# Token attention's last two units on VectorE, edge sends moved out of the last unit, feed-forward constants loaded ahead

## The reference, cut to what matters

```python
x = _layernorm(x + _L0_attn_ref(x, ...))        # attention across tokens
x = _layernorm(x + _L0_xattn_ref(x, ctx, ...))  # the two attentions below
x = _layernorm(x + _L0_ffn_ref(x, ...))         # feed-forward, 8 experts
x = _layernorm(x + _L1_attn_ref(x, ...))        # Nystrom attention, graph edges
x = _layernorm(x + _L1_xattn_ref(x, ctx, ...))
x = _layernorm(x + _L1_ffn_ref(x, ...))
```

```python
# 16 heads of 64, SCALE = 1/8, x1 the tokens, out = x1 + the first block on ctx
dots = jnp.einsum('bhid,bhjd->bhij', q, k) * SCALE
attn = jax.nn.softmax(dots, axis=-1)
out  = jnp.einsum('bhij,bhjd->bhid', attn, v)
return out @ Wo + bo
# feed-forward
x_attn = _layernorm(x_flat, ln_g, ln_b) @ attn_w + attn_b + x_flat
h = gelu(einsum(g, w1) + b1); y = einsum(h, w2) + b2
out = gelu(y @ next_w + next_b)
```

## Time and profile before

| | |
|---|---|
| median of 3 runs | 2498.34 us (2494.76 to 2500.62) |
| profiled execution | 2499.3 us, its span 2497.5 us |
| busy: TensorE, VectorE, ScalarE, GpSimd | 92%, 61%, 44%, 43% of the span |
| mean granted clock of TensorE | 0.956 of full speed |
| chain that ended last, largest part | TensorE 29% of the span |

### The profile page before, as it was taken

How to read it: one execution, slowest core, us unless ns; L and a number is a source line. 1 busy time by engine, 2 the same in 40 slices (tenths; PEclk the granted TensorE clock), 3 DMA queues, 4 the chain that set the end, 5 groups by cost and what they waited for, 6 DMA issues and landing times. The chain is left out here.

```text
span 2497.5 us, 34571 instructions
## 1 busy us (share of the span) xinstructions
PE 2295.9 (92%) x12918; PEld 1436.2 (58%) x12918; DVE 1520.1 (61%) x2287; ACT 1104.7 (44%) x2354; POOL 1079.6 (43%) x785
## 2 busy tenths in 40 slices
PE   6999999879988999998899999799899589979998
PEld 3333343356764555554555554688666467768887
DVE  6778678447745666764666666632444556666556
ACT  2667557723322444442344444233321457643233
POOL 2556546513443788883478888133301122100000
PEclk7889989999999999999999999899999699989999
DMA  6454333223110111112011111254201141010001
GB/s 131 114 97 87 70 65 76 77 57 62 1 18 1 10 15 14 15 31 39 1 14 11 15 15 14 80 133 126 61 25 45 32 115 52 1 64 14 1 1 34
DMA packets 137615, 114.22 MB, mean 46 GB/s; under 512 B 74501, under 2 KB 114931, under 8 KB 137065
## 3 DMA queue, kind: packets, MB, share of 16 engines
q1 hardware_dynamic: 100297, 111.08, 16.5%
q0 software_dynamic: 36864, 0.15, 4.4%
q10 hardware_dynamic: 288, 0.79, 0.2%
HBM read 85.99 MB, written 13.39 MB: 40 GB/s over the span
## 5 line engine op out<-in xcount | busy, mean ns | idle before, releaser
L345 POOL DMA_INDIRECT adj<-e_EE,e_IX x256 | 421.1, 1645 | 437.8 <-DMA adj<-e_EE,e_IX 346.5
L1799 DVE TENSOR_REDUCE c_MX<-PS 128x2 f32<-128x1024 f32 x256 | 312.9, 1222 | 175.6 <-PE PS L120 174.5
L124 POOL TENSOR_TENSOR c_AC<-c_AC,c_P 128x1024 f32<-128x1024 f32 x150 | 380.9, 2539 | 78.9 <-DVE c_AC L124 71.7
L1896 ACT ACTIVATE c_P<-PS 128x1024 f32<-128x1024 f32 x256 | 252.3, 1026 | 224.7 <-PE PS L120 216.6
L733 DVE TENSOR_REDUCE a_MX<-PS 128x2 f32<-128x1024 f32 x256 | 303.7, 1220 | 64.2 <-PE PS L120 61.9
L839 ACT ACTIVATE a_P<-PS 128x512 f32<-128x512 f32 x512 | 270.6, 601 | 95.9 <-PE PS L120 93.6
L120 PE MATMUL PS<-c_P,c_VV 128*64 128x512 f32 x1024 | 247.7, 605 | 0.0
L129 POOL TENSOR_SCALAR e_EQ<-e_KR,e_KC 128x128 bf16<-128x128 f32 x256 | 162.9, 636 | 160.9 <-DMA e_KR<-adj_key 125.1
L120 PE MATMUL PS<-a_QS,a_KS 64*128 64x512 f32 x512 | 197.4, 468 | 19.3 <-ACT a_P L839 8.5
L120 PEld LDWEIGHTS PS<-a_QS,a_KS 64*128 64x128 f32 x512 | 85.5, 193 | 174.4 <-ACT a_P L839 95.8
L120 PE MATMUL PS<-a_KS,a_QS 48*128 48x512 f32 x512 | 174.0, 482 | 11.6 <-DVE a_MX L733 4.6
(11 more groups left out here) (499 smaller groups left out, 4608.5 us busy)
## 6 DMA issues: line engine op xcount, KB each, us to landing
e_KR<-adj_key SPq DMA_DIRECT2D x64, 256.0 KB, 3.5
f_W<-in_L_ffn_w SPq DMA_DIRECT2D x16, 1024.0 KB, 6.9
c_RB<-c_r SPq DMA_DIRECT2D x58, 128.0 KB
g_FB<-in_fside_1x16xSxS SPq DMA_DIRECT2D x8, 616.0 KB, 8.0
a_QS<-a_QH SPq DMA_DIRECT2D x32, 128.0 KB
adj<-e_zt SPq DMA_DIRECT2D x16, 256.0 KB, 4.2
adj<-e_EE,e_IX POOLq DMA_INDIRECT x256, 3.2
d_AJ<-adj SPq DMA_DIRECT2D x8, 512.0 KB, 7.0
```

The lines of the kernel that those rows point to most:

```text
L124: return v.e.tensor_tensor(o, a, b, op)
L345: g.e.indirect_dma_start(self.adj, bass.IndirectOffsetOnAxis(ap=self.IXE[:, k:k + 1], axis=0), self.EE[:, k:k + 1], None, compute_op=ALU.a ...
L1799: v.e.reduce_max(MX[:, w % 2, :, qt, kh], bank(0, 2).rearrange("p (h n) -> p h n", h=2), AX, negate=True).then_inc(*smax_dve.up())
L1896: s.e.activation(PB[t % NP][:, :, :].rearrange("p h n -> p (h n)"), bank(2 + 2 * (t % 2), 2), ACT.Exp, scale=0.125).then_inc(*st_act.up())
```

## The change

- `lead(w)` gives 7 also for unit 30: VectorE makes all seven additions of units 15, 30 and 31. The additions 5 and 6 of unit 30 are placed at n = 0 and 1 of unit 31.
- The sum of unit 30 is made at n = 3 of unit 31 in place of n = 5, its scaling at n = 6 in place of 7.
- No sends in unit 31; one after each of `out` 9 to 15 instead.
- f_CR and f_AW now lie over LS and are loaded by SyncE at n = 6 of unit 31, once all queries have been prepared; `stage_f` allocates and loads neither.

```diff
     def lead(w):
-        return 7 if w % 16 == 15 else 2
+        return 7 if direct(w) else 2
...
-                    if n == 0 and not first:
+                    if n == 0 and not first and lead(w - 1) < 7:
                         yield "acc", w - 1, 7
+                    if w == 31 and n < 2:
+                        yield "add", 30, 5 + n
...
-                    if n == 7 and w == 31:
+                    if n == 6 and w == 31:
                         yield "scale", 30
+                        yield "fetch", 3
...
-                    if n == 5 and not first:
+                    if n == (3 if w == 31 else 5) and not first:
                         yield "sum", w - 1
...
-                    if n in (1, 3, 5):
+                    if n in (1, 3, 5) and w < 31:
                         yield "send", 1
...
         for t in range(9, 18):
             if t < 16:
                 yield "out", t
+                yield "send", 1
...
             elif kind == "fetch":
                 n, = a
-                if n == 1:
+                if n == 3:
+                    sp.wait_ge(q_pe, 32)
+                    K.consts.load(sp, A)
+                elif n == 1:
...
+class Consts:
+    def __init__(self, K):
+        self.CR = K.over("f_CR", "LS", 0, [84, 128], F32)
+        self.AW = K.over("f_AW", "LS", 512, [128, 2, 256], F32)
+        self.cr_in, self.aw_in = K.lasting(16), K.lasting(16)
+
+    def load(self, sp, A):
+        for place, name in ((slice(0, 64), "L0_ffn_b1"), (slice(64, 80), "L0_ffn_b2")):
+            dma(sp, self.CR[place, :], A[name].rearrange("e (f p) -> (e f) p", p=128)).then_inc(*self.cr_in.up())
+        for place, name in ((slice(80, 82), "L0_ffn_ln_g"), (slice(82, 84), "L0_ffn_ln_b")):
+            dma(sp, self.CR[place, :], A[name].rearrange("(f p) -> f p", p=128)).then_inc(*self.cr_in.up())
+        dma(sp, self.AW[:, :, :], A["L0_ffn_attn_w"].rearrange("(c p) n -> p c n", p=128)).then_inc(*self.aw_in.up())
...
-    AW = sb(c, "f_AW", [128, 2, 256])
-    CR = sb(c, "f_CR", [84, 128])
+    CR, AW = K.consts.CR, K.consts.AW
+    cr_in, aw_in = K.consts.cr_in, K.consts.aw_in
...
-        dma(sp, CR[0:64, :], A["L0_ffn_b1"].rearrange("e (f p) -> (e f) p", p=128)).then_inc(*cr_in.up())
-        dma(sp, CR[64:80, :], A["L0_ffn_b2"].rearrange("e (f p) -> (e f) p", p=128)).then_inc(*cr_in.up())
-        dma(sp, CR[80:82, :], A["L0_ffn_ln_g"].rearrange("(f p) -> f p", p=128)).then_inc(*cr_in.up())
-        dma(sp, CR[82:84, :], A["L0_ffn_ln_b"].rearrange("(f p) -> f p", p=128)).then_inc(*cr_in.up())
-        load("L0_ffn_attn_w", AW[:, :, :], aw_in)
```

More of the change, by code:

```diff
@@ L2040, in stage_f @@
     TM = sb(c, "f_TM", [128, 4, 256])
-    CR = sb(c, "f_CR", [84, 128])
     CC = sb(c, "f_CC", [128, 84])
-    aw_in, cr_in, rows_in, nw_in, ahead_in = [K.landing() for _ in range(5)]
+    CR, AW = K.consts.CR, K.consts.AW
+    cr_in, aw_in = K.consts.cr_in, K.consts.aw_in
+    rows_in, nw_in, ahead_in = [K.landing() for _ in range(3)]
     w1_in = [K.landing() for _ in range(2)]
@@ L3436, in build @@
             K.fine_out = K.lasting(16)
+            K.consts = Consts(K)
             stage_ctx(K, block, "b_", 0.125, K.W0, True)
```

## The result

The kernel after took 2483.4 us (median of 9 runs, 2475.3 to 2489.5), the kernel before 2494.8 us in the same nine rounds (2490.9 to 2501.2). The two medians lie 11.4 us apart; the ratio, which goes by all these runs, is 0.9948, 95% interval 0.9933 to 0.9962: 13.0 us less, between 9.5 and 16.7. Measured a second time with new runs the ratio was 0.9950 (0.9935 to 0.9965). The kernel is faster, by about the 11.9 us forecast or a little more.

The account below looks back on a forecast made before the run. The prediction took GpSimd's queue to bound the end of units 30 and 31. Its terms, 8.2 + 2.1 + 0 + 0 + 1.6 = 11.9 us, taken off 2498.34, gave 2486.4 us, range 2482 to 2491.

Parts of the forecast that it names:

- The releaser: End of the second batch, units 30 and 31: GpSimd's queue, not TensorE, owns the stretch and releases output projection tile 8.
- Step 2: TensorE in unit 31: output projection tile 8 starts at 1559.05 in place of 1567.25, 8.2 us won.
- Step 3: Output projection tile 8 runs at full clock, 3.62 instead of 5.85 us: 2.1 us won, ends 0 and 2.2.
- Step 1: Unit 30's five adds go from GpSimd to VectorE: 6.1 us there, ending near 1541, 1545.6 at worst.
- step 4: VectorE's reciprocal of unit 30 comes before unit 31's last six adds: cost 0, at worst 0.5 us.
- Step 5: Three sends leave unit 31, seven go into the tail, 43 instead of 44 in feed-forward: 0, ends 0 and 0.9 us gain.
- Step 6: Start of feed-forward: f_CR and f_AW loaded ahead, first projection at 1609.5 instead of 1611.12; 1.6 us won, ends 0.4 and 3.7.
- B: Output projection tile 8 comes earlier but the clock falls before or at it: 8.1 us won, 2490.2 us; chance 0.12.
- C: VectorE becomes the bound in unit 31, only 1.6 us stay: 2496.7 us; chance 0.07 together with E.
- E: GpSimd still releases output projection tile 8, as unit 29's scaling gets its input late; chance 0.07 together with C.
- D: Clock stays at 1.2 GHz in feed-forward: 11.2 us slower, 2509.5 us; chance 0.03.

Follow-up runs that it names:

- the adds alone: Kernel before with only unit 30's adds moved from GpSimd to VectorE; ratio 0.9960 (0.9946 to 0.9973), 10.0 us less.

## Why the prediction was right, and where not

**The releaser.** Right. GpSimd's queue owned the stretch; with its adds gone TensorE has no wait, as the adds alone show.

**Step 2, out 8 at 1559.05.** Measured 1558.88 on the same clock. **Step 3, the tile at full clock.** 3.72 us by its row. Together they were to give 10.3 us, and T shrank by 10.5 against the trace on which the sum was made. But that sum was true of one course of the old kernel. Against its two other traces (89.5 us) the same change wins 6.7 to 6.8: out 8 comes 6.8 us sooner in place of 8.2, and step 3 gives nothing, since out 8 was at the full clock there already. Step 3 had a lower end of 0, but for a clock that falls in the new kernel too, not for an old kernel that doesn't lose it there; and step 2 had no range at all.

**Step 1 and step 4, VectorE.** The five adds took 7.7 us, within the 6.1 to 11.0 that the two ends given for them mean; the reciprocal of unit 29 ran at 1541.91, and c_RB followed 1.4 us later than before on the same clock, harmless as said. The six adds ended 1.1 us before they were asked for; 0.2 us too late had been the worst case. Cost 0, as taken.

**Step 5, the sends.** The seven fit (six waits of 1.8 us between them, the last from 1588.97 on), 43 were sent in feed-forward. Taken as 0, and nothing shows another value. What the prediction missed is that the sends win something by themselves (T 3.6 us shorter than in the later traces of before), so that their move was insurance against the adds' failing.

**Step 6, the constants.** 1.6 us forecast. The two traces of the forecast give 2.7: a 0 came 2.2 us sooner after SyncE's first issue in place of 1.6, and one slow tile fewer gave the rest, within the upper end of 3.7. The other pairs give 1.0 to 2.3, the mean over all traces 1.7, so the term stands.

**The time: the step that failed.** The mechanism held; what was mis-sized is the last term, the level from which the gain is taken off. The 2486.4 us rest on 2498.34 us, the median of three runs, and the range allowed "a microsecond for the median of few runs". Nine, thirty-five, seventeen and eleven runs later gave 2494.8, 2494.8, 2496.0 and 2493.6: the level was 2.4 to 4.7 us too high, 3.6 in the rounds of the result. From 2494.8 us the same sum gives 2482.9, and its range would have begun at 2478.9. The measured median of 2483.4 us lies in the range of 2482 to 2491, but the ratio applied to the level of its own rounds, 2494.76 x 0.9948, gives 2481.8, just below it. That the stated time was missed by only 3 us is no proof of the level. The gain, 11.9 us forecast, was 13.0 and 12.5; since the traces make steps 2 and 3 worth 10.5 us in one course of the old kernel and 6.7 to 6.8 in the other, how near it came is in part luck.

**What stays open.** From the last c_XH matmul to the end of feed-forward the three traces of before took 265.8, 260.8 and 262.1 us, the two of after 252.5 and 252.3: 10.5 us by their means. The runs say 12.5 to 13. Between lie 2 to 2.5 us that no trace places. One reading is that the costlier course of the old kernel is commoner in whole runs than in its three traces, for the adds alone won 10.0 us in whole runs and the change without the constants 10.2, near the 10.3 of the first trace; against it stands that only one of the six traces with the old queue took that course. And the unchanged stages scatter by more than 2.5 us (graph attention between 159.4 and 168.0 over all traces, the part before the last c_XH matmul by 7.8 in three traces of one kernel), and the intervals reach down to 8.7 and 9.5, so chance may be all of it. Neither is shown.

Of the rivals, B (the clock falls before out 8 all the same) and C (VectorE the bound) didn't happen, nor did E, since GpSimd's scaling of unit 30 ended at 1554.57. D (a clock that stays low) didn't happen either: it rose after two tiles. But the prediction is wrong that nothing in this trace shows a clock low for tens of microseconds. The first stage of the kernel before does, with TensorE at work (columns of the earlier trace rows):

```profile
49.20:76.60 27.40, 23.92 (x75) 10.69 (x73) 22.02 (x21) 7.02 (x18) 8.71 (x14) 0.50 0.45 126
```

## What to carry to other kernels

Where one queue releases the bounding engine, parts of it are not worth the sum of what each wins alone (by T against the later traces: sends 3.6, adds 6.5, both 6.8), so price them together and take the set that leaves slack for the others. A wait of TensorE can cost twice, the second time through its clock, but only where the slow work lies on the path: 2.1 us at out 8, nothing under the P·V of unit 31. Which of them it is changes from run to run, so take more than one trace of the kernel before. A stretch without such waits wins steadiness too (T within 0.3 us, where it was within 3.8). A forecast in microseconds needs a margin for the level of before, which three runs don't fix.

## What was unexpected of the hardware

The same program lost its clock at different places: 3.21 and 1.50 us for a P·V and a sum and 3.72 for out 8 in one run, 1.94, 1.03 and 5.85 in another, with GpSimd's adds and scaling the same and one of its sends 0.5 us longer. And filling three small gaps (1.73, 0.61 and 1.54 us of products of ones) held the granted clock at 1.00 through a stage change that otherwise ran at 0.61 to 0.80 of full speed between the last c_OT and the first f_AW matmul.
